# Three scalar loads on another queue, one PSUM pair exchanged, one subtraction moved ahead

## What is computed

```python
def fake_quant(x, scale, zp):
    q = clip(round(x / scale + zp), 0, 255)
    return (q - zp) * scale

# layer 1
x = x + tanh(g_xattn) * (fake_quant(layernorm(x), x1_scale, x1_zp) @ fake_quant(ctx, x2_scale, x2_zp))
# layer 2, on t = layernorm(x)
scores = softmax(t @ router_w + router_b) + router_bias     # best 2 of 4 groups, then best 2 of 16 experts
y = sum over the chosen e of gate[e] * ((silu(t @ ew1[e] + eb1[e]) * (t @ ew2[e] + eb2[e])) @ ew3[e] + eb3[e])
z = (silu(t @ sw1 + sb1) * (t @ sw2 + sb2)) @ sw3 + sb3     # shared expert, inner width 512
x = x + tanh(g_ffn) * (y + z)
```

## Time and profile before

| | us |
|---|---|
| median of 3 runs | 317.61 (316.82 to 317.87) |
| the profiled execution, its own time | 318.93 |
| its span, first to last instruction | 317.0 |
| PE busy in it | 294.3 |
| DVE busy | 222.6 |
| ACT busy | 115.1 |
| POOL busy | 25.3 |

### The profile page before, as it was taken

The page is one execution under the profiler, slowest core; times in us unless marked ns, Lnnn a source line. Parts: engine busy times, 40 slices in busy tenths (PEclk is TensorE's granted clock), DMA queues, the critical chain, the costliest instruction groups (busy, mean ns, idle before and its releaser), DMA issues.

```text
span 317.0 us, 4650 instructions
## 1 busy us (share of the span) xinstructions
PE 294.3 (93%) x1868; PEld 149.5 (47%) x1868; DVE 222.6 (70%) x392; ACT 115.1 (36%) x130; POOL 25.3 (8%) x34
## 2 busy tenths in 40 slices
PE   0398998989999999999999999999999999999993
PEld 0234598954444444644444444444444444444441
DVE  2898987895698863686465988877794859759210
ACT  1898558759562450200352404402006040100000
POOL 2010201000001310000000021101101110000000
PEclk9999999999999999999999999999999999999997
DMA  7999260249940555000698420000000000500302
GB/s 280 413 323 319 69 196 7 83 144 219 340 149 0 96 104 132 2 2 0 189 316 292 173 95 2 0 0 0 2 0 0 2 1 0 237 31 1 132 33 103
DMA packets 34164, 35.56 MB, mean 112 GB/s; under 512 B 16068, under 2 KB 28380, under 8 KB 34012
## 3 DMA queue, kind: packets, MB, share of 16 engines
q1 hardware_dynamic: 34128, 35.23, 35.7%
q10 hardware_dynamic: 12, 0.00, 0.0%
HBM read 27.88 MB, written 4.20 MB: 101 GB/s over the span
## 4 chain that ended last, share of the span: by engine, by line
PE 80%; DVE 11%; ACT 3%; DMA 2%; issue 1%; POOL 1%; ACTq 0%; DVEq 0%
PE PS L1526 26%; PE PS L1367 20%; PE PS L1559 11%; PE PS L1552 7%; PE PS L1402 7%; PE PS L1314 4%; DVE stats L771 3%; DMA sc<-in_g_ffn_dram 2%; PE PS L1321 1%; DVE X L837 1%; PE PS L1383 1%; DVE S2f L807 1%; DVE areaW L820 1%; POOL lnR L471 1%; DVE wrow L846 1%
## 5 line engine op out<-in xcount | busy, mean ns | idle before, releaser
L1367 PE MATMUL PS<-areaT,areaW 128*128 128x512 f16 x288 | 62.6, 379 | 1.1 <-DVE SA L851 1.1
L1367 PEld LDWEIGHTS PS<-areaT,areaW 128*128 128x128 f16 x288 | 27.9, 98 | 34.6 <-DVE SA L851 1.3
L1526 PE MATMUL PS<-areaT,area 128*128 128x512 f16 x192 | 42.1, 379 | 0.0
L1526 PE MATMUL PS<-areaT,areaW 128*128 128x512 f16 x192 | 42.1, 379 | 0.0
L1314 PE MATMUL PS<-area,areaQ 128*128 128x512 f16 x128 | 32.2, 402 | 1.8 <-DVE area L803 1.1
L1035 DVE SCALAR_TENSOR_TENSOR X<-PS,cf,X 128x512 f32<-128x512 f32 x22 | 15.5, 745 | 20.0 <-PE PS L1559 15.2
L1526 PEld LDWEIGHTS PS<-areaT,areaW 128*128 128x128 f16 x192 | 18.8, 98 | 22.6
L1526 PEld LDWEIGHTS PS<-areaT,area 128*128 128x128 f16 x192 | 18.8, 98 | 22.6
L771 DVE BATCH_NORM_STATS2 stats<-X 128x6 f32<-128x512 f32 x32 | 20.5, 684 | 4.3 <-DMA X<-in_x_dram 4.1
L1552 PE MATMUL PS<-SW,areaH 128*128 128x512 f16 x96 | 21.9, 379 | 0.0
L1314 PEld LDWEIGHTS PS<-area,areaQ 128*128 128x128 f16 x128 | 12.7, 103 | 18.1 <-issue 3.6
(11 more groups left out here) (187 smaller groups left out, 411.9 us busy)
## 6 DMA issues: line engine op xcount, KB each, us to landing
ring<-in_L_ffn_sw_dram SPq DMA_DIRECT2D x12, 512.0 KB, 5.1
X<-in_x_dram SPq DMA_DIRECT2D x8, 512.0 KB, 7.4
areaT<-in_ctx_dram SPq DMA_DIRECT2D x8, 512.0 KB, 8.6
ring<-in_ctx_dram SPq DMA_DIRECT2D x8, 512.0 KB, 4.0
ring<-in_L_ffn_ew_dram SPq DMA_DIRECT2D x16, 256.0 KB, 5.5
out_dram<-X SPq DMA_DIRECT2D x7, 512.0 KB, 2.7
ring<-in_L_ffn_ew_dram SPq DMA_DIRECT2D x2, 1024.0 KB, 4.9
areaQ<-gate_dram SPq DMA_DIRECT2D x1, 1024.0 KB, 6.4
```

What stands on the lines that cost most here:

```text
L1367: last = mm(PS[:, SU_BANK[half * SC + c] + w, lo:hi], SW[:, wp, 2 * c + w, k, :], XT[:, xp, k, tk], start=(k == 0 and n == 0), stop=(k == ...
L1526: last = mm(PS[:, EU_BANK[u] + w, :], W12S[j][:, wp, k, cs], XT[:, xp, k, b * S:(b + 1) * S], start=(k == 0 and n == 0), stop=(k == KC - 1 ...
```

## The change

Three things change.

1. ACT issues the loads of the first three scalars only. POOL issues the other three, ahead of its constants, with a semaphore `small_in2` of their own. DVE waits for both.
2. The third shared block of batch 0 (c = 2) goes to banks 0 and 1, and the fourth (c = 3) to banks 4 and 5. Blocks 2 and 3 then need other waits: block 2 waits for none of `su_hf`, block 3 for the first gate. The products of tile 4 (banks 0 and 1) wait for the third gate, where they waited for the moved tokens of batch 0. Tile 6 (banks 4 and 5) waits for the fourth gate, one tile sooner than before, when tile 6 waited for the third and tile 7 for the fourth.
3. DVE makes the low half of tile 2 ahead of the statistics of tile 3, no longer behind them.

```diff
-        SU_BANK = (4, 6, 4, 6, 4, 2, 6, 4)
+        SU_BANK = (4, 6, 0, 4, 4, 2, 6, 4)
...
         def _(pool):
+            for n, s in ((3, x2_zp), (4, g_xattn), (5, g_ffn)):
+                pool.dma_start(sc1[n:n + 1, 0:1], s.rearrange("(a n) -> a n", a=1)).then_inc(small_in2, 16)
...
-            for n in range(len(scalars)):
+            for n in range(3):
                 act.dma_start(sc1[n:n + 1, 0:1], scalars[n].rearrange("(a n) -> a n", a=1)).then_inc(small_in, 16)
...
-            dve.wait_ge(small_in, 96)
+            dve.wait_ge(small_in, 48)
+            dve.wait_ge(small_in2, 48)
...
             attend(3)
+            ln2_lo(2)
             bn(3)
-            ln2_lo(2)
...
-                if half == 0 or c == 3:
-                    pe.wait_ge(su_hf, half * SC + (c - 1 if half == 0 else 1))
+                if c == 3:
+                    pe.wait_ge(su_hf, half * SC + 1)
...
                 if i == TB:
-                    pe.wait_ge(tk_hi, TB)
-                    pe.wait_ge(tk_lo, TB)
+                    pe.wait_ge(su_hf, SC - 1)
                 if i == TB + 1:
                     pe.wait_ge(r1_rdy, B)
-                if i >= TB + 2:
-                    pe.wait_ge(su_hf, i - TB + 1)
+                if i == TB + 2:
+                    pe.wait_ge(su_hf, SC)
```

More of the change, by code:

```diff
@@ L211, in build @@
         c0_in = [sem(f"c0_in{i}") for i in range(KC)]
-        small_in, bias_in = sem("small_in"), sem("bias_in")
+        small_in, small_in2, bias_in = sem("small_in"), sem("small_in2"), sem("bias_in")
         sc_wide, sc_T, sc_rdy = sem("sc_wide"), sem("sc_T"), sem("sc_rdy")
```

## The result

The changed kernel takes 320.51 us, the median of 5 runs (317.69 to 321.39), beside 317.36 us (316.79 to 317.87) for the kernel before in the same comparison. The ratio is 1.0082, with a 95% interval of 1.0049 to 1.0115: slower, where 316.8 us and most likely no change had been forecast, and above the range's upper end of 318.4. A repetition, against its own runs of the kernel before, gave 1.0051 (1.0030 to 1.0071).

What follows compares the result with a forecast made beforehand. PE bounds the kernel, its products of tile 4 at 88.83 us held by a context chain of DVE, SP's queue and DMA. Banks 0, low half 0.4 and scalars 0.4 gain 0.8 us: 317.61 to 316.8 us, range 316.2 to 318.4.

Steps and rivals of the forecast that it cites:

- The bound and the banks: Tile 4's products at 88.83 us wait for the last context sum, so removing PE's 1.10 us wait at 66.55 gains 0.
- the prediction's own signs: Timeline checks; the prediction is wrong if the last context sum moves by much more or less than 0.8 us.
- The low half: Tile 2's low half ahead of tile 3's statistics: PE starts sooner, gain 0.4 us, bounded by 0 and 0.43.
- The scalars: Three scalar loads on POOL at the start: DVE's wait to 7.45 us shortens, gain 0.4, bounds +0.57 and -1.2.
- a landing at 7.0 us: When POOL's scalar loads were assumed to be in, against DVE's wait ending at 7.45 us: a gain of 0.4.
- the far bound: POOL's third load issued at 3.7 us after 1.5 us per issue, landing at 8.7: a loss of 1.2 us.
- The clock: Slow rival: PE's clock falls in the longer idle time before tile 4's products; 318.5 us, chance 0.20.
- the number of 8 slow matmuls: Matmuls of tile 4 assumed at half clock, picked between 0 and 12: price 8 x 0.21 = 1.7 us.
- the 0.20: Chance given to PE's clock falling in the idle time ahead of tile 4's products.
- some 2.1 us: Idleness of PE that can make the clock fall, taken from the end of the program in the kernel before.
- The row sums are work of a kind: Argument against a clock fall before tile 4's products: one-column matmuls count as work, leaving 1.7 us of proper idleness.
- Both slow rivals: PE's clock falling before tile 4's products (318.5 us, chance 0.20); POOL's scalar loads landing after 7.45 us (318.4 us, 0.12).

Runs made afterwards that it cites:

- b_banks: Kernel before with only the PSUM banks of blocks 2 and 3 and their waits changed: 1.0009 (0.9976 to 1.0043), median 319.25 us.
- f_perk: Changed kernel, but tile 4's products wait for each clamped context row by itself, only the column sums for the sum of all: 0.9960 of the kernel before.
- c_low: Kernel before with only tile 2's low half moved ahead of the statistics of tile 3: 1.0009 (0.9992 to 1.0027), median 317.89 us.
- a_scalars: Kernel before with only the scalars changed, three of them on POOL's queue: 1.0030 (1.0010 to 1.0050), 12 runs.
- g_perk_act: Changed kernel with row-by-row waits for tile 4's products and all six scalars on ACT's queue: 0.9941 (0.9924 to 0.9957) of the kernel before.
- h_bc: Kernel before with banks and low half changed, the scalars left on ACT's queue: 1.0009 (0.9984 to 1.0034), median 318.17 us.
- j_split42: Changed kernel with row-by-row waits for tile 4's products, four scalars on ACT's queue and two on POOL's: 0.9937 (0.9919 to 0.9955) of the kernel before.
- before: The kernel before the change, with nothing edited: 317.36 us (316.79 to 317.87) in the first comparison.
- d_after: The changed kernel itself run again, against new runs of the kernel before: 1.0051 (1.0030 to 1.0071), median 319.77 us.
- e_fill: Changed kernel plus six unused 512-column matmuls behind the row sums of batch 1: 1.0005 (0.9983 to 1.0027) of the kernel before, median 319.04 us.

## Why the prediction was wrong

**The bound and the banks: right in mechanism.** The forecast had the products of tile 4 hang on the last context sum, and the removed 1.10 us worth 0. The trace after has the sum at 88.05 against 88.04, `b_banks` has the products at 88.92 against 88.83, and `f_perk` shows the converse: with that wait gone from ahead of the products they follow the row sums at once. Tiles 5 and 6 brought no new wait. But the last context sum, which was to move by 0.8 us, did not move in the first trace, and by the prediction's own signs that is where it fails: in the terms for the low half and the scalars, which were to move it.

**The low half: right in size, by one trace.** Its wait was forecast at 0.65 us and measured 0.69; the term was 0.4 us, and the products moved by 0.32 in `c_low`. The times neither show nor exclude it.

**The scalars: wrong in sign. This is the first step that failed.** I took a landing at 7.0 us, "nearer to ACT's rows since the packets wait in any queue behind the same large loads", and priced the term at +0.4. The third POOL load landed at 8.0. What I had as the far bound (a landing at 8.7 and a loss of 1.2 us) was the nearer one, though its construction was wrong: the issues took 0.52 to 0.73 us each, not 1.5, and the delay is behind the issue, 5.5 us, where the bound had 5.0. It is not one unlucky trace. In the five profiled executions with three on POOL the copy starts at 7.80 to 8.47 us, mean 8.05; in the six with all on ACT at 6.72 to 7.45, mean 6.99. The 7.45 that I took as "all that this part can win" was itself the latest of the six. Step and price together: a gain of 0.4 us forecast, a loss of 0.95 measured (`a_scalars`), or of 0.6 (`f_perk` against `g_perk_act`).

Nor would a landing at 7.0 have been sure to pay. The prediction had x tile 2 in at 13.9 us, by one trace, and a start of its statistics 0.37 us sooner. In `b_banks` and `h_bc`, whose start is that of the kernel before, the copy stood at 6.72 and 6.82 us, yet these statistics came at 14.67 and 14.68, behind waits of 1.05 and 0.95 us for the tile: later than the 14.27 of the earlier trace rows.

The Trainium skill's figures ("DMA: Bandwidth & Descriptors", Latency and other measured facts), by which I had an estimate of 6.7 us, were further off than my own. Landings 4.1, 4.8 and 5.5 us after issues 0.72 and 0.52 us apart are not latencies of about 1 us. I read them as loads that queue behind large ones, and `j_split42` (7.19 us with two on POOL) fits, but no run separated this from the 32 packets that each takes.

**The clock: the mechanism was there, the chance was not.** The price was forecast at 1.7 us and measured 1.66. That it came so near is in part luck: the number of 8 slow matmuls was picked between 0 and 12. The idle stretch, forecast at 1.7 us, was 1.52 and 2.33 us in the two traces of this kernel. There was no fall behind 1.52 us, nor behind 1.74 in `b_banks`; there was one behind 2.33. What failed is the 0.20. I read one profiled execution's times as the kernel's. The idle stretch differed by 0.8 us between two traces of the same kernel, by a load's landing, so that its length in one says little of how often the clock falls: 11 of 17 executions of the changed kernel have the lower mean.

Nor does the length alone decide. I took "some 2.1 us" from one fall, at the end of the kernel before. The end of the changed kernel's first trace, where PE has no work left either, is the counterexample:

```profile
311.65:315.80 4.15, 0.00 (x0) 0.00 (x0) 0.75 (x1) 0.00 (x0) 0.00 (x0) 1.00 0.20 69
```

Here the clock stayed full for 4.15 us without work. At the ends of other traces it fell 2.2 us (`before`), 2.3 us (`c_low`), 3.7 us (`a_scalars`) and 4.5 us (`b_banks`) after the last matmul. So an idle stretch makes a fall possible, and one trace does not give its chance. "The row sums are work of a kind" is neither borne out nor refuted: in `d_after` the clock fell some 2.3 us after them, a time at which it also fell behind full-width matmuls. `e_fill`, which left 0.51 us of the gap, had 1 fall in 12 for 7 in 12.

**The range.** Both slow rivals came true at once. I had priced each as the only thing to go wrong, at 318.5 and 318.4 us, and so ended the range at 318.4. Neither excludes the other. The forecast itself had been given a smallest gain of 0.3 us, though the bounds stated for its terms, 0 for the low half and a loss of 1.2 for the scalars, reach to 318.8.

**The sum, by what was measured.** In us added to the time: scalars 0.95, low half -0.3, banks 0, clock 1.56 x 7/12 = 0.9, together 1.55. The clock's term is taken from `d_after` itself; without it the sum is 0.65, and its five other executions lie 0.7 above the 318.32 of those of the kernel before that did not fall. `d_after` measured 0.0051 x 318.48 = 1.6 us. In the first comparison, 4 of 5 executions fell and two of them to 0.987 and 0.989, and it measured 2.6 us.

**What stays open.** The changed kernel fell in 11 of 17 executions, `b_banks` and `h_bc` together in 6 of 24. The late scalars may be what separates them, but no run shows how: with three on POOL the idle stretch was 1.52 and 2.33 us, without them 1.62 (`h_bc`) and 1.74 (`b_banks`). And the executions of `b_banks` at 0.986 and 0.989 cost 2.5 and 3.2 us, more than the one fall that a trace shows. A mean of 0.987 over 319 us is, as an estimate, some 8 us at half clock, where the 0.993 of `d_after`'s trace is 4.5; whether they fall twice or stay low for longer is not known. Why POOL's loads land late is open too.

## What to carry to other kernels

Before taking away a wait, look at the next one behind it and at what ends that, in more than one trace. If another chain ends it, the time comes back there, and two short idle times that become one long one can cost the clock as well. Then split the next wait too (for the row, not for all rows): here the two edits that gave nothing alone gave 0.5% on top of the 0.1% of the split wait (0.9941 against 0.9988). A load of a few bytes that something early waits for belongs by its landing and not by its issue: move it and look at what lands later in its place. And when two rivals point the same way, the range must hold their sum.

## What the runs showed of the hardware

- A 4-byte load issued by POOL moved 32 packets, one issued by ACT 2; with large loads under way POOL's landed 4.1 to 5.9 us after their issue, in the six traces that have them.
- TensorE's granted clock went from full to 0.50 at the end of an idle time of 2.33 us behind 0.94 us of one-column matmuls (`d_after`), and was full again from 93 us on while PE was busy. Sixteen wide matmuls took 5.27 us in place of 3.61.
- With no work left for PE at the program's end, the granted clock fell 2.2 us after the last matmul in one trace and 4.5 us after it in another, and in a third it stayed full for the 4.15 us to the end.
- The kernel with three 4-byte loads on SP's queue measured 0.9902 with them behind the first context row and 0.9961 with them ahead of it. The statistics of x tile 2 started at 13.50 and 14.83 us in their traces.
- The last store, 256 KB, landed 2.9 us after its issue in one profiled execution and 4.1 in another, a difference larger than the change's whole forecast.
